# Attention between two feed-forward halves: end redrawn with two buffers of sums, first iteration's quads stored apart

## What is computed

```python
x = x + 0.5 * ffn(LN(x))          # ffn(z) = z @ W.T + b + (z @ V_r) @ C.T, rank 32
x = x + attn(LN(x))               # 16 heads of 16, causal
x = x + 0.5 * ffn(LN(x))
# attn: qkv = z @ W_attn; s = q.k / 4; masked with -inf above the diagonal
# p = (1 - 0.01 s if -100 <= s <= 0;  s*s + 1 if s > 0;  else 0) / 1000;  y = p @ v;  y @ W_proj
```

## Time and profile before

| | us |
|---|---|
| median of 3 executions | 1956.75 (1953.23 to 1956.96) |
| the profiled execution | 1957.39 |
| its span, first to last instruction | 1955.6 |
| TensorE busy | 1667.1 |
| VectorE busy | 1328.0 |
| ScalarE busy | 1363.4 |
| GpSimd busy | 1323.8 |

### The profile page before, as it was taken

The page is one execution under the profiler, slowest core; times in us unless marked ns, Lnnn a source line. Parts: engine busy times, 40 slices in busy tenths (PEclk is TensorE's granted clock), DMA queues, the critical chain, the costliest instruction groups (busy, mean ns, idle before and its releaser), DMA issues.

```text
span 1955.6 us, 66923 instructions
## 1 busy us (share of the span) xinstructions
PE 1667.1 (85%) x27158; PEld 807.2 (41%) x27158; DVE 1328.0 (68%) x3313; ACT 1363.4 (70%) x2178; POOL 1323.8 (68%) x1419
## 2 busy tenths in 40 slices
PE   4687889898989899898989989898988889898884
PEld 2344334343434444353444435343444444434332
DVE  1465677776767777677777767777677777777652
ACT  1244568787878777777778778776877888886650
POOL 3354558787878767778776768877677767676552
PEclk9898889999999999999999999999999999999996
DMA  2343433332315242343424333341513231413111
GB/s 74 122 135 120 128 102 93 93 104 79 112 50 152 67 118 76 113 117 90 121 59 129 92 101 102 95 133 32 159 50 118 70 95 49 117 39 106 37 36 58
DMA packets 155190, 183.14 MB, mean 94 GB/s; under 512 B 22012, under 2 KB 129660, under 8 KB 152836
## 3 DMA queue, kind: packets, MB, share of 16 engines
q1 hardware_dynamic: 154884, 178.82, 31.3%
HBM read 102.43 MB, written 76.30 MB: 91 GB/s over the span
## 4 chain that ended last, share of the span: by engine, by line
PE 52%; ACT 17%; DVE 15%; issue 8%; POOL 4%; DMA 3%; SPq 0%; ACTq 0%; DVEq 0%; POOLq 0%
PE y_ps L977 19%; PE score L977 16%; PE bank L977 13%; DVE rp L912 9%; ACT rp L820 7%; ACT rp L836 4%; PE bank L1003 3%; ACT rp L840 3%; POOL z L686 2%; DVE lin L918 1%; DMA part_scratch<-parts 1%; ACT lin L826 1%; DVE qk_max L924 1%; DMA out_dram<-x 1%; DVE bnst_ln L937 1%
## 5 line engine op out<-in xcount | busy, mean ns | idle before, releaser
L912 DVE TENSOR_SCALAR rp<-score 128x512 f32<-128x512 f32 (+2 forms) x1728 | 944.2, 574 | 223.4 <-PE score L977 219.7
L977 PE MATMUL score<-qs,ks 96*32 96x512 bf16 (+3 forms) x10240 | 742.8, 354 | 169.5 <-DVE rp L912 86.1
L724 POOL TENSOR_TENSOR rp<-rp 128x1024 f32<-128x1024 f32 (+1 forms) x416 | 755.7, 1828 | 148.5 <-DVE rp L912 137.2
L820 ACT ACTIVATE rp<-score 128x512 f32<-128x512 f32 (+1 forms) x832 | 458.5, 592 | 292.3 <-PE score L977 289.8
L977 PE MATMUL y_ps<-rp,vt 128*16 128x512 f32 (+3 forms) x5120 | 598.6, 539 | 22.1 <-ACT rp L840 14.2
L977 PEld LDWEIGHTS score<-qs,ks 96*32 96x32 bf16 x10240 | 291.6, 96 | 599.0 <-DVE rp L912 314.1
L836 ACT ACTIVATE rp<-rp,rise 128x1024 f32<-128x1024 f32 (+1 forms) x416 | 464.1, 1145 | 1.4 <-POOL rp L699 1.4
L699 POOL TENSOR_SCALAR_AFFINE_SELECT rp<-rp 128x256 f32<-128x256 f32 (+1 forms) x384 | 184.1, 481 | 312.6 <-ACT rp L820 158.4
L840 ACT ACTIVATE rp<-rp 128x1024 f32<-128x1024 f32 (+2 forms) x224 | 291.1, 1305 | 121.3 <-POOL rp L699 67.6
L918 DVE SCALAR_TENSOR_TENSOR lin<-score,slope_mask 128x128 f32<-128x128 f32 x768 | 215.1, 280 | 0.0
L977 PEld LDWEIGHTS y_ps<-rp,vt 128*16 128x16 f32 x5120 | 133.6, 97 | 102.4 <-ACT rp L840 25.5
(11 more groups left out here) (78 smaller groups left out, 1392.9 us busy)
## 6 DMA issues: line engine op xcount, KB each, us to landing
part_scratch<-parts SPq DMA_DIRECT2D x16, 1536.0 KB, 7.5
qs<-part_scratch SPq DMA_DIRECT2D x384, 64.0 KB
ks<-part_scratch SPq DMA_DIRECT2D x384, 64.0 KB, 2.4
state_scratch<-st_new SPq DMA_DIRECT2D x16, 528.0 KB
st<-state_scratch SPq DMA_DIRECT2D x64, 132.0 KB
x_sb<-in_L_attn_x_dram SPq DMA_DIRECT2D x16, 512.0 KB, 4.3
x_scratch<-x SPq DMA_DIRECT2D x16, 512.0 KB, 5.3
qT_scratch<-qkT SPq DMA_DIRECT2D x16, 512.0 KB, 3.9
```

The costliest lines, as they stand in the source:

```text
L724: pool.tensor_tensor(half, half, half, ALU.mult).then_inc(squared["pool"], 1)
L820: nc.scalar.activation(rp[T % RP_BUFS][:, 2 + v, off:CH], score[H % S_BUFS][:, v, off:CH], ACT.Relu).then_inc(raised["act"], 1)
L912: nc.vector.tensor_scalar(rp[T % RP_BUFS][:, 2 * u + v, off:CH], score[H % S_BUFS][:, v, off:CH], 0.0, RISE, ALU.max, ALU.add).then_inc(ra ...
L977: return nc.tensor.matmul(*args, start=start, stop=stop, skip_group_check=True)
```

## The change

Six things are changed. (1) Constants have signals of their own: identity, ffn weights, bias, w_qkv, w_out; x is loaded first and w_in last of the ffn weights; four buffers are filled by DVE instead of GpSimd; ScalarE empties w_ffn at the first z1T's slot instead of ahead of all. (2) kT stands behind the next chunk's z1T, at slots 14 and 15 of a stretch instead of 30 and 32, ffn, v and ln2 two slots later. (3) The first iteration's halves start at slot 28 of the first stretch (64 instead of 96) and are spread from window to window. (4) For chunks 0 to 3, q and k of the first quads (parts of block 0) are stored by DMAs of their own, SyncE waits for each and loads them at once; qT and v of quad 0 are copied from SBUF to SBUF; state is loaded when stored; the rest of parts is stored by itself. (5) Loads of v, qT and state have signals of their own. (6) x2 has two buffers, and stage C is placed anew: chunks 8 and 9 in iteration 12, 10 in 13, 11 in 14, 12, 13 and 14 from slots 1388, 1418 and 1428, 15 from 1460, with 12 slots between the last scores and it. Added waits guard the new reuse (scales for the last z, GpSimd's z3 for the last z3T, q's and v's emptying for the direct copies and loads).

```diff
-A_EARLY = {"z1T": (12, 13), "ffn": (14, 18), "z2T": (38, 39), "ln1": 0, "ln2": 22}
-B_EARLY = {"qT": (0, 2), "k": (4, 8), "v": (22, 26), "kT": (30, 32), "state": (31, 33, 34, 35)}
+A_EARLY = {"z1T": (12, 13), "ffn": (16, 20), "z2T": (38, 39), "ln1": 0, "ln2": 24}
+B_EARLY = {"qT": (0, 2), "k": (4, 8), "kT": (14, 15), "v": (24, 28), "state": (32, 33, 34, 35)}
+C_HALF = {"proj": (0, 6), "ln3": 10, "z3T": (24, 26), "out": (28, 34)}
+C_LATE = {"proj": (0, 4), "ln3": 8, "z3T": (20, 21), "out": (22, 26)}
 C_SHORT = {"proj": (0, 4), "ln3": 8, "z3T": (20, 21), "out": (22, 26)}
+HALVES_AFTER = 28
...
     o.stage(0, at, A_FIRST)
-    at = o.stretch(40)
-    o.stage(0, at, B_EARLY)
-    o.stage(1, at, A_EARLY)
-    for c, (length, first) in enumerate(((40, 20), (40, 14), (44, 14), (48, 14))):
-        at = o.stretch(length, spread(first, length, 2 * (LAST[c] + 1 - FIRST[c])))
-        o.stage(c + 1, at, B_EARLY)
-        o.stage(c + 2, at, A_EARLY)
+    starts = []
+    for c, length in enumerate((40, 40, 40, 44, 48)):
+        at = o.stretch(length)
+        o.stage(c, at, B_EARLY)
+        o.stage(c + 1, at, A_EARLY)
+        starts.append(at + HALVES_AFTER)
+    starts[CPB] = o.n
+    for c in range(CPB):
+        o.put_halves(spread(starts[c], starts[c + 1], 2 * (LAST[c] + 1 - FIRST[c])))
     for n in range(1, ITERS):
         at = o.stretch(NHALF, range(NHALF))
         if n + CPB < NCH:
             o.stage(n + CPB, at, B_FULL)
         if n + CPB + 1 < NCH:
             o.stage(n + CPB + 1, at, A_FULL)
-        if CPB <= n < ITERS - 1:
+        if CPB <= n < ITERS - CPB:
             o.stage(n - CPB, at, C_FULL)
-    o.stage(NCH - 5, at, C_SHORT)
-    o.stage(NCH - 4, at + 27, C_SHORT)
-    o.stage(NCH - 3, at + 54, C_SHORT)
+        if n == ITERS - CPB:
+            o.stage(n - CPB, at, C_HALF)
+            o.stage(n - CPB + 1, at + NHALF // 2, C_HALF)
+        if ITERS - CPB < n < ITERS - 1:
+            o.stage(n - CPB + 1, at, C_FULL)
+    for c, s in ((NCH - 4, 20), (NCH - 3, 50)):
+        o.stage(c, at + s, C_SHORT)
     assert o.next_half == ITERS * NHALF
     o.drain = o.n
-    o.stretch(LAG + 2)
-    o.stage(NCH - 2, o.stretch(32), C_SHORT)
-    o.stage(NCH - 1, o.stretch(40), C_SHORT)
+    o.stage(NCH - 2, at + 60, C_LATE)
+    o.stretch(LAG + 9)
+    o.stage(NCH - 1, o.stretch(32), C_SHORT)
...
-        x2 = sb("x2", [P, NB, DM])
+        x2 = [sb(f"x2_{i}", [P, NB, DM]) for i in range(2)]
...
-            sp.dma_start(w_in[:], ffn_w.rearrange("(k p) d -> p k d", p=P)).then_inc(w_loaded, 16)
             sp.dma_start(x_sb[:], x_d[0:CH, :].rearrange("(i p) d -> p i d", p=P)).then_inc(x_loaded, 16)
-            sp.dma_start(vr_in[:], ffn_v.rearrange("(k p) r -> p k r", p=P)).then_inc(w_loaded, 16)
-            sp.dma_start(c_in[:], ffn_c.rearrange("(k p) r -> p k r", p=P)).then_inc(w_loaded, 16)
-            sp.dma_start(bias_half[:], ffn_b.rearrange("(a n) -> a n", a=1).broadcast_to([P, DM])).then_inc(w_loaded, 16)
-            sp.dma_start(w_qkv[:], w_attn.rearrange("(k p) n -> p k n", p=P)).then_inc(w_loaded, 16)
-            sp.dma_start(w_out[:], w_proj.rearrange("(k p) n -> p k n", p=P)).then_inc(w_loaded, 16)
-            sp.wait_ge(const_ready, 5)
+            sp.dma_start(vr_in[:], ffn_v.rearrange("(k p) r -> p k r", p=P)).then_inc(ffn_loaded, 16)
+            sp.dma_start(c_in[:], ffn_c.rearrange("(k p) r -> p k r", p=P)).then_inc(ffn_loaded, 16)
+            sp.dma_start(w_in[:], ffn_w.rearrange("(k p) d -> p k d", p=P)).then_inc(ffn_loaded, 16)
+            sp.dma_start(bias_half[:], ffn_b.rearrange("(a n) -> a n", a=1).broadcast_to([P, DM])).then_inc(bias_loaded, 16)
+            sp.dma_start(w_qkv[:], w_attn.rearrange("(k p) n -> p k n", p=P)).then_inc(qkv_loaded, 16)
+            sp.dma_start(w_out[:], w_proj.rearrange("(k p) n -> p k n", p=P)).then_inc(out_loaded, 16)
+            sp.wait_ge(filled, 1)
             for b in range(BATCH):
                 sp.dma_start(st_d[b, 0], st_new[:, 0, :]).then_inc(st_zero, 16)
-            sp.wait_ge(st_zero, 16 * BATCH)
...
-                    if x.chunk < CPB:
-                        put(x.empty_at + 5, "kq", 0, x.chunk)
+                if x.chunk < CPB:
+                    if (x.kind, x.i) == ("qT", 0):
+                        put(x.empty_at + 2, "first q", x.chunk)
+                    if (x.kind, x.i) == ("kT", 0):
+                        put(x.empty_at + 2, "first k", x.chunk)
+                    if (x.kind, x.i) == ("v", 1):
+                        put(x.empty_at + 1, "first v", x.chunk)
+                    if (x.kind, x.i) == ("state", NB - 1):
+                        put(x.empty_at + 7, "first st", x.chunk)
                 if (x.kind, x.i) == ("proj", 0):
-                    put(max(x.start - 12, o.again if x.chunk >= NCH else 0), "c", x.chunk)
+                    last_y = o.copy_slot[(x.chunk // CPB * QUADS + QUADS - 1) * CPB + x.chunk % CPB] if x.chunk < NCH else o.again
+                    put(max(x.start - 12, last_y + 1), "c", x.chunk)
                 if (x.kind, x.i) == ("out", 1):
                     put(x.empty_at + 1, "out", x.chunk)
             for n in range(ITERS):
                 for c in range(CPB):
-                    put(o.copy_slot[n * CPB + c] + 1, "y", n, c)
+                    at.setdefault(o.copy_slot[n * CPB + c] + 1, []).insert(0, ("y", n, c))
...
+                        if b >= CPB:
+                            sp.dma_start(part_d[b].rearrange("p w g s t -> p (w g s) t"),
+                                         parts[:].rearrange("p g s t -> p (g s) t")).then_inc(parts_stored, 16)
+                        else:
+                            sp.dma_start(part_d[b, :, :, 1].rearrange("p w s t -> p w (s t)"),
+                                         parts[:].rearrange("p (w k) s t -> p w k (s t)", k=KC)[:, :, 1, :]).then_inc(parts_stored, 16)
+                    if what == "first q":
+                        c, = args
+                        cols = slice(CH * c, CH * c + CH)
+                        if c == 0:
+                            sp.wait_ge(filled, FILLED)
+                        wait_emptied(sp, "qT", c, 0)
+                        sp.dma_start(qT[1:QD + 1, cols], qkT[0:QD, 0, :]).then_inc(qT_loaded[c], 16)
+                        sp.wait_ge(split_step, 12 * c + 3)
+                        sp.dma_start(part_d[c, :, 0, 0], parts[:, 0, :, :]).then_inc(first_q_stored, 16)
+                        sp.wait_ge(first_q_stored, (c + 1) * 16)
+                        load_q(0, c, q_loaded[c])
+                    if what == "first k":
+                        c, = args
+                        sp.wait_ge(split_step, 12 * c + 9)
+                        sp.dma_start(part_d[c, :, 1, 0], parts[:, KC, :, :]).then_inc(first_k_stored, 16)
+                        sp.wait_ge(first_k_stored, (c + 1) * 16)
+                        load_k(0, c, k_loaded[c])
+                    if what == "first v":
+                        c, = args
+                        wait_emptied(sp, "v", c, 1)
+                        sp.dma_start(vt[:, NB * c:NB * c + NB, :], v_sb[:, 0, :, :]).then_inc(v_loaded[c], 16)
+                    if what == "first st":
+                        c, = args
+                        sp.wait_ge(st_zero, 16 * BATCH)
+                        sp.wait_ge(st_stored, (c + 1) * 16)
+                        load_st(0, c, st_loaded[c])
                     if what == "q":
                         n, c = args
                         all_stored(n // QUADS * CPB + c + 1)
                         sp.wait_ge(qk_done, 2 * (2 * ((n - 1) * NT + LAST[c]) + 2))
                         sp.wait_ge(pv_done, (n - 1) * NT + FIRST[c] + 1)
                         load_q(n, c, q_loaded[c])
+                        load_qT(n, c, qT_loaded[c])
+                        load_st(n, c, st_loaded[c])
                     if what == "k":
                         n, c = args
                         sp.wait_ge(pv_done, (n - 1) * NT + KEY_LAST[c] + 1)
                         load_k(n, c, k_loaded[c])
+                        load_v(n, c, v_loaded[c])
...
-            pool.wait_ge(w_loaded, 16 * 6)
-            pool.wait_ge(const_ready, 14)
-            pool.tensor_scalar(bias_half[:], bias_half[:], 0.5, 0.0, ALU.mult, ALU.add).then_inc(const_ready, 1)
-            pool.wait_ge(const_ready, CONSTS)
+            pool.wait_ge(bias_loaded, 16)
+            pool.tensor_scalar(bias_half[:], bias_half[:], 0.5, 0.0, ALU.mult, ALU.add).then_inc(bias_loaded, 1)
+            pool.wait_ge(bias_loaded, 17)
...
+            def empty_weights():
+                for k in range(KC):
+                    act.wait_ge(setup_pe, 2 + k)
+                    nc.scalar.activation(w_ffn[:, k, :], y_ps[k][:, 0:DM], ACT.Copy, scale=0.5).then_inc(setup_act, 1)
+                act.wait_ge(const_ready, CONSTS)
+                act.wait_ge(filled, FILLED)
...
+                        if a <= CPB:
+                            act.wait_ge(v_loaded[a - 1], 16)
...
```

(29 more changed lines are left out.)

90 lines of the change are left out of this document (55 added, 35 removed).

## The result

The changed kernel takes 1985.79 us (median; 1982.71 to 1987.77) against 1956.86 beside it: a ratio of 1.0146, 95% interval 1.0131 to 1.0162. It is 29 us **slower**, where 1923.5 was forecast. The profiled execution took 1982.7 us, its span is 1981.0.

A forecast was written before the change was run, and what follows sets the result against it. Two ends were taken as chains, not engine-bound, around an unchanged middle; -10.8 - 0.4 - 16.6 - 6.1 = -33.9 from 1957.4 us gave 1923.5, own range 1912 to 1936, full range 1904 to 1941.

The forecast's parts named there:

- The start: Setup before the first z1T: own signals and DVE fills let z's transposes start near 14.0 instead of 24.76, -10.8 us.
- The store wait: First iteration: ScalarE's three waits for the parts store (22.2 us) go, worth 5.1, 5.3 and 6.2 us.
- first stretch: First iteration's opening stretch: -5.1 store wait, +3.8 for 3 halves, +2.6 key wait, -1.7 splits, together -0.4 us.
- The new wait for keys: Chunk 0, SyncE's store and load round trip: TensorE waits 2.6 us (0 to 9); later chunks have cover.
- rival (d): Slower: SyncE's queue is the bound, first keys reach TensorE late in all four chunks, 1967 us; chance 0.04.
- The halves move forward: First iteration's later stretches: earlier score halves shorten 217.3 to 200.7 us, -16.6, store waits included (-26 to -8).
- price list: Old stretches without waits: 8, 16, 24, 38 halves take 34.7, 43.0, 55.8, 72.3 us, 1.0 to 1.6 a half.
- The middle: Iterations after the first and before the end: left alone by the change, periods of 112.6 us unchanged.
- the splits of chunk 0: First iteration: two moved splits beside GpSimd's bias adds can add up to 1.5 us to the wait for keys.
- The end: Iterations 12 to 15 and after: last copy +7.3 us, behind it 37.0 against 50.4 (-13.4), together -6.1.
- Rival (b): The end gives back: C costs 9.4 in iteration 12, crowding its upper bound; end +4 instead of -6, 1934; chance 0.10.
- The loads' price: Stage C loads at the end: chunk 14's +4.5 us (0 to 8), chunk 12's +1.

The follow-up runs named there:

- The experiment with the early state: Changed kernel with the first iteration's state of windows 2 and 3 loaded early from chunk 0's stored state (another sum computed): 1969.56 us, ratio 1.0083.
- repaired: Changed kernel with v, qT and state on shared signals from iteration 1 on and first-iteration halves from slot 36 instead of 28: 1933.22 us, ratio 0.9906.
- slot 40: Changed kernel with shared signals from iteration 1 on and first-iteration halves from slot 40 of their stretches instead of 28: 1926.84 us, ratio 0.9878.

## Why the prediction was wrong

**The start** (-10.8): right. z1T came 10.1 us earlier in the changed kernel; alone, the start gained 10.3 in the median. The fills on DVE took 5.5 us, between the bounds.

**The store wait**: right that the three waits go. That 5.1, 5.3 and 6.2 us of the time go with them was not borne out (the first is a term of the first stretch, the other two are 11.5 of the 16.6 below): with the halves in their old place the first iteration takes 269.1 us from z1T on without the waits, and 268.3 to 275.9 with them. **The new wait for keys** (2.6 us in chunk 0): 2.4, and none in later chunks, so rival (d)'s place was wrong too. But behind the first half came what the first stretch did not count: GpSimd's masks and square of the early halves stood ahead of three of the four parts of chunk 1's second z, and TensorE waited for it:

```profile
70.77 1.94 PE L1097 MATMUL bank<-ident,z 128*128 128x128 f32 x8 [5.19 <-POOL z L764]
```

Before, it waited 1.73 us at this place, for DVE's part of the state sum. Stretch one was 4.2 over.

**The halves move forward** (-16.6, and the range to -8): this step failed. It read a price for each half off the old stretches, where no half waited for a load, and applied it to halves that stand ahead of their inputs. (Read off in straight lines, the same price list gives 203.1 and not 200.7 us, so -14.2.) It asked of the keys whether they come in time, and not of the state, though by the change "state is loaded when stored". Two slots were to be compared, the first values' and the state's load, both in the order: 154 against 158, and 196 against 198. The 10.06 us are 3.4 until the state's store is issued, 4.25 until its load is issued and 2.45 until TensorE goes on; with the round trip of 6 us that the prediction itself gave the keys, two waits of 6 to 10 us would have come out, enough to turn -33.9 into -14 to -22. The experiment with the early state gives 18.8 us for them. The rest was not taken apart. The clock granted in the stretches after is 0.78 to 0.84 in four of five (0.83 to 0.91 in the earlier trace rows), which goes with TensorE's longer idle times; what it costs by itself no run shows. Even repaired, the new first iteration closes at 281.0 at slot 36 (269.6 at 40) against 285.1 with the old one and the new start: 4 us, which is within what single profiles differ by, or 15 at slot 40, where 17 were forecast. The medians, 1933.22 and 1926.84 against 1935.14, give 2 and 8.

**Rival (d)** named the right queue and the right kind of failure, SyncE's round trips behind the state's store, but put it on the keys, in four chunks. It is the linear part, in two. It had 0.04.

**The middle** ("periods of 112.6 unchanged", "around a middle that the change leaves alone"): this step failed. It went by the bytes and by who waits: no load was late, so signals of their own cost nothing. The three waits a window on TensorE's queue moved DVE's shift from 0.12 us ahead of GpSimd's square to 0.09 behind it, and 24.0 us followed. The prediction applied the rule of the shared ports to the splits of chunk 0, where it allowed 1.5 us and none was blocked (each rest 0.68 us; later ones took up to 2.02 us, and up to 2.34 before), and did not look for two-input operations in the steady state, where a race could be lost once an iteration. That it would be lost could not be read from the trace of before; that 0.12 us stood between the two, and that it had been lost in iteration 5 (1464 ns), could, and a rival for it was due. Iteration 5's own loss was 1.2 us, so ten of them would have been 12 us, half of what came.

**The end** (-6.1): iteration 12 +10.4 (forecast +9.4), 13 and 14 -1.3, 15 -6.7, so the last copy moved by +2.4 (bounds +2 to +15) instead of +7.3. (Rival (b) took the upper bound of +15 and wrote +4 for the end; with it the end is 15 - 13.4 = +1.6.) The loads' price was right in sum, 5.4 us measured for 5.5, though split otherwise: chunk 12's took 3.57 instead of 1, chunk 14's 1.86 instead of 4.5. The third row is chunk 15's projection:

```profile
1846.60 1.08 PE L1072 MATMUL bank<-w_out,y_c 128*32 128x256 f32 x8 [3.57 <-DMA x1c<-x_scratch]
...
1908.86 0.64 PE L1072 MATMUL bank<-w_out,y_c 128*32 128x256 f32 x8 [1.86 <-DMA x1c<-x_scratch]
...
1953.82 5.33 PE L1072 MATMUL bank<-w_out,y_c 128*32 128x256 f32 x64 [7.20 <-DMA x1c<-x_scratch]
```

What shortened iteration 15 beyond the forecast was not taken apart. Behind the last copy 38.2 us, forecast 37.0: the projection of 15 starts 11.0 behind it (10.3) and takes 5.33 (4.2).

In sum: -10.8 became -10.1, the first stretch and the halves (-17.0) became +21.3, the middle 0 became +24.0, the end -6.1 became -9.8: +25.4, which is the difference of the spans (1981.0 - 1955.6).

## What to carry to other kernels

When an order is drawn anew, every input of a moved step is checked by its slot: a step that is priced by its neighbours' mean price is priced with its inputs present. A wait that is always met still moved what stands behind it, here by 0.2 us, and where two engines share a resource by whoever comes first, that decided 1.2 us of VectorE and up to 3 of the period in each iteration; so in a regular loop one looks for short two-input DVE operations within a few tenths of a microsecond of a GpSimd operation, and prices the lost race times the iterations. Parts of a large change are worth measuring by themselves: here two of them brought 16 us together, and the whole change cost 29, each against the kernel before beside it, so the others cost 45. And a wait that a change removes is worth what the next thing in line leaves of it: here 20 us of ScalarE's waits went, and the first iteration was no shorter for it.

## What the hardware showed unexpectedly

A DVE operation of 128x4 elements with two SBUF inputs, 0.16 us long, took 1.28 to 1.46 us behind a GpSimd product that had started 0.20 to 0.02 us earlier, and ended with it. The same work with one SBUF tensor and a value for each lane was never blocked (112 instructions of 202 to 216 ns, 45 of them begun during a GpSimd product). DVE's 1.17 us at a place where it had just been waiting made a period 2.1 us longer. DVE fills 66x2048 float32 in 1.76 us and 128x1040 in 0.93.
